# The SiLU after the convolutions: one ScalarE operation in place of tanh and a product

## The chip, the cores and the metric

One NeuronCore of a Trainium2 chip runs the whole program: TensorE (PE: matmuls), VectorE (DVE), ScalarE (ACT: functions through tables), GpSimd (POOL), and SyncE (SP), which issues the DMAs. The metric is the device time of one execution, in microseconds.

## The reference

Two layers on 1024 tokens of width 512: gated linear attention, a router that mixes expert biases, a state-space mixer with a depthwise convolution, and low-rank adapters. The change is in the mixer's convolution:

```python
hBC = proj[..., INTER:INTER + CONV_DIM]          # INTER 8192, CONV_DIM 8192 + 2048
xc = conv_general_dilated(transpose(hBC), conv_w, ..., feature_group_count=CONV_DIM)   # 4 taps, causal
xc = xc + conv_b[None, :, None]
hBC = jax.nn.silu(transpose(xc))                  # silu(x) = x * sigmoid(x)
hs = hBC[..., :INTER]                             # 128 heads of 64: the x channels
Bm, Cm = ...                                      # 8 groups of 128 each: the B and C channels
Y = scores(Cm, Bm) * decay @ (hs * dt) + ...      # in chunks of 128 tokens
out = grouped_rms(Y * silu(gate)) @ out_proj_w
```

## The kernel before

Every matrix product in fp32 is three passes over a high and a low part: ScalarE copies a weight chunk to `slab_hi` (`split_hi`, L190), VectorE subtracts to get `slab_lo` (`split_lo`, L199 or L201), and TensorE runs 12 matmuls of 128x512 per unit (`unit`, L216 to L218). Each engine executes its own list in order. Semaphores tie the lists together: `wait_ge` on one side, `then_inc` on the other.

A convolution of a unit (128 channels, 512 tokens) is `conv_start` on ScalarE (L1182: the fourth tap and the bias, from PSUM to an `acc` buffer) and then three operations of VectorE (`conv_taps`, L1192), each of which adds a tap. The weights and bias are halved on their way in, so that `acc` holds x/2. SiLU(x) is then acc * (1 + tanh(acc)): a tanh on ScalarE into a second buffer, and a product either on VectorE (one operation, L1268, L1625) or on GpSimd (two operations, L1279 and L1282, L1671 and L1674).

`bc_phase` (B and C channels) has 32 units: a loop of two turns, in each two slabs of eight units. The products of even units are on GpSimd, those of odd ones on VectorE. Its results go to DRAM (`bc_scratch`), and the mixer starts after the last of these stores.

`mixer_phase` runs over 8 groups (a loop of 7 turns, and the last written out), each in two halves s = 0 and s = 1, each half in 24 slots. Slots 0 to 7 project and convolve the x units (x0 to x7); slots 8 to 23 project gates and outputs. In slots 4 to 11, TensorE transposes the eight convolved units (L1433) and ScalarE copies each from PSUM to `mx_HS` (L1525); the transposes of slot n + 1 wait for the copy of slot n. From slot 8 on, ScalarE also computes the decays: for two banks a Relu (L1534) and an Exp (L1536), which VectorE multiplies (L1615). It also computes the gate's tanh (L1551) and, for the norm, a Square (L1519). In slots 1 to 8, ScalarE's list has the tanh of the previous slot's unit at the slot's end (L1563). Six of the products in a half are on GpSimd, the last two on VectorE.

Of the kernel before, what the change touches and what calls it, by code (L numbers as in the profile page):

```python
# [59 lines left out]
def alone(eng):  # L60


    eng.nop(nofuse=True)
# [26 lines left out]
def build(nc, d, out):  # L90
# [76 lines left out]
    + ["bc_ld", "bc_a", "bc_tap", "bc_th", "bc_p", "bc_cm", "bc_st0", "bc_st1", "bc_st2", "bc_st3"]  # L167
    + ["mx_ld", "mx_zero", "mx_set", "mx_bc", "mx_row0", "mx_row1", "mx_a", "mx_tap", "mx_th", "mx_cm", "mx_hsT", "mx_pt", "mx_hs",
# [1027 lines left out]
def bc_phase(nc, K, d, scratch):  # L1196
# [6 lines left out]
    th = [mem.enter_context(nc.sbuf_tensor(f"bc_th{i}", [P, HALF], F32)) for i in range(2)]  # L1203
# [30 lines left out]
    def _(act):  # L1234
        with act.Fori(0, 2) as i:
            for j in range(2):
                for u in range(9):
# [9 lines left out]
                    if u > 0:  # L1247
                        act.wait_ge(S["bc_tap"], HEAD + 3 * n)
                        act.wait_ge(S["bc_cm"], HEAD + n - 2)
                        nc.scalar.activation(th[(u - 1) % 2][:, :], acc[(u - 1) % 4][:, :], ACT.Tanh).then_inc(S["bc_th"], 1)  # L1250

    @block.vector
    def _(dve):
        with dve.Fori(0, 2) as i:
            for j in range(2):
                for u in range(9):
# [7 lines left out]
                    if u > 0 and u % 2 == 0:  # L1264
                        dve.wait_ge(S["bc_th"], HEAD + n)
                        dve.wait_ge(S["bc_cm"], HEAD + n - 1)
                        a = acc[(u - 1) % 4][:, :]
                        nc.vector.scalar_tensor_tensor(a, th[(u - 1) % 2][:, :], 1.0, a, ALU.add, ALU.mult).then_inc(S["bc_cm"], 1)  # L1268

    @block.gpsimd  # L1270
    def _(pool):
        with pool.Fori(0, 2) as i:
            for u in range(0, 16, 2):
                n = 16 * i + u
                pool.wait_ge(S["bc_th"], HEAD + n + 1)
                pool.wait_ge(S["bc_cm"], HEAD + n)
                alone(pool)
                a, w = acc[u % 4][:, :], th[u % 2][:, :]
                nc.gpsimd.tensor_tensor(w, w, a, ALU.mult).then_inc(S["bc_p"], 1)  # L1279
                pool.wait_ge(S["bc_p"], HEAD + 8 * i + u // 2 + 1)  # L1280
                alone(pool)
                nc.gpsimd.tensor_tensor(a, w, a, ALU.add).then_inc(S["bc_cm"], 1)  # L1282
# [4 lines left out]
def mixer_phase(nc, K, d, rows, scratch, dtk, from_start, to_end, out):  # L1287
# [17 lines left out]
    POOL_SILU = 6  # L1305
# [6 lines left out]
    with ExitStack() as mem:  # L1312
# [13 lines left out]
        th = sb("th", [P, HALF])  # L1326
# [6 lines left out]
        TH = [th, TO]    # L1333
# [165 lines left out]
        def _(act):  # L1499
            act.wait_ge(S["mx_set"], HEAD + 1)  # L1500

            def half(g, s, last):
                q = 2 * g + s
                n, u0, m = N + 3 * q, U + SLOTS * q, T + NT * q
                for sl, (kind, i) in enumerate(units):
# [50 lines left out]
                    if 1 <= sl < 9:  # L1556
                        act.wait_ge(S["mx_tap"], HEAD + 3 * (NT * q + sl))
                        act.wait_ge(S["mx_cm"], HEAD + NT * q + sl - 2)
                        if sl == 1:
                            act.wait_ge(S["mx_q"], HEAD + NT * q)  # L1560
# [347 lines left out]
```

## Time and profile before

| | us |
|---|---|
| median of 3 runs | 2725.96 (2719.48 to 2730.78) |
| the profiled execution | 2725.1 |
| its span | 2723.4 |
| TensorE busy | 2566.6 |
| VectorE busy | 1877.7 |
| GpSimd busy | 1460.6 |
| ScalarE busy | 1349.5 |
| B/C stage, about | 995 to 1100 |
| mixer, about | 1100 to 2610 |

The profile is that of one execution. TensorE is the busiest engine, and each other engine is busy for half to two thirds of the span. The B/C stage is where TensorE has its longest run of waits for VectorE. A half of the mixer takes about 94 us. Numbers behind a row in brackets are idle time of the engine just before, and who ended it.

### The profile page before, as it was taken

The page shows a single profiled execution, that of the slowest core. Times are in us where ns is not written, and L with a number is a line of the kernel's source. Part 1 is how long each engine was busy: PE and PEld are TensorE (multiplying, and loading weights), DVE is VectorE, ACT ScalarE, POOL GpSimd, SP SyncE. Part 2 cuts the span into 40 slices and gives each one's busy share as a digit, 9 for nine tenths or more (in the row PEclk, how much of TensorE's full clock was granted, in tenths as well). Part 3 has the DMA queues.
Part 4 walks back from the last instruction along what each step waited for, and adds up shares of the span by engine and source line. Part 5 has one row for each costly group of instructions (what it writes and reads, how often), then busy time and mean ns, then how long its engine had stood idle before and what let it go on. Part 6 is the DMA issues. An engine that isn't in the chain of part 4 may idle for free.

```text
span 2723.4 us, 59094 instructions
## 1 busy us (share of the span) xinstructions
PE 2566.6 (94%) x19678; PEld 2041.8 (75%) x19678; DVE 1877.7 (69%) x2744; ACT 1349.5 (50%) x2481; POOL 1460.6 (54%) x1428
## 2 busy tenths in 40 slices
PE   4999999999999679799999999999999999999989
PEld 3778787787787456677777777777777777777777
DVE  5675666766757679757667777587576677775874
ACT  3434434434334255456564664665565646656621
POOL 1654655556546113457556656576575566575720
PEclk8999999999999879899999999999999999999999
DMA  2010010110110023211111111101111111111011
GB/s 89 24 50 29 32 46 24 40 40 23 47 36 12 15 93 112 72 45 38 50 33 58 34 42 50 36 31 50 45 37 51 33 54 34 45 49 38 18 47 47
DMA packets 72663, 119.04 MB, mean 44 GB/s; under 512 B 10310, under 2 KB 22214, under 8 KB 72373
## 3 DMA queue, kind: packets, MB, share of 16 engines
q1 hardware_dynamic: 72388, 115.61, 12.9%
q8 instruction: 144, 2.36, 0.4%
q14 instruction: 131, 1.07, 0.1%
HBM read 102.92 MB, written 12.65 MB: 42 GB/s over the span
## 4 chain that ended last, share of the span: by engine, by line
PE 47%; DVE 4%; issue 4%; POOL 2%; ACT 2%; DVEq 0%; ACTq 0%; POOLq 0%; DMA 0%; SPq 0%
PE proj L216 10%; PE proj L218 10%; PE proj L217 10%; PE core_y L1406 5%; PE core_o L1412 2%; PE turned L250 2%; DVE mx_acc L1192 2%; PE turned L1433 2%; PE decay L1465 1%; PE mx_decay L1465 1%; POOL mx_acc L1674 1%; PE mx_decay L216 1%; PE mx_decay L217 1%; PE mx_decay L218 1%; POOL mx_th L1671 1%
## 5 line engine op out<-in xcount | busy, mean ns | idle before, releaser
L216 PE MATMUL proj<-slab_hi,XTL 128*128 128x512 f32 x816 | 354.6, 435 | 0.0
L199 DVE TENSOR_TENSOR slab_lo<-slab_raw,slab_hi 128x512 fp32r<-128x512 f32 (+2 forms) x272 | 256.8, 956 | 133.5 <-ACT slab_hi L190 108.1
L216 PE MATMUL proj<-XTH,slab_lo 128*128 128x512 f32 x736 | 299.6, 407 | 44.8 <-PEq L81 18.5
L218 PE MATMUL proj<-slab_hi,XTH 128*128 128x512 f32 x816 | 320.2, 392 | 0.0
L217 PE MATMUL proj<-slab_lo,XTH 128*128 128x512 f32 x816 | 318.4, 390 | 0.0
L218 PE MATMUL proj<-XTH,slab_hi 128*128 128x512 f32 x736 | 291.9, 397 | 0.0
L217 PE MATMUL proj<-XTL,slab_hi 128*128 128x512 f32 x736 | 291.4, 396 | 0.0
L1688 POOL TENSOR_TENSOR mx_gate<-mx_gate,mx_hd 128x512 f32<-128x512 f32 x128 | 171.2, 1337 | 156.0 <-DVE mx_hd L1602 145.0
L216 PE MATMUL proj<-slab_hi,mx_otl 128*128 128x512 f32 x576 | 242.0, 420 | 0.0
L218 PE MATMUL proj<-slab_hi,mx_oth 128*128 128x512 f32 x576 | 227.7, 395 | 0.0
L217 PE MATMUL proj<-slab_lo,mx_oth 128*128 128x512 f32 x576 | 227.2, 394 | 0.0
L951 POOL TENSOR_TENSOR at_ropeA<-at_ropeA,at_ropeB 128x512 f32<-128x512 f32 x80 | 110.6, 1383 | 206.6 <-DVE at_ropeB L896 206.6
L190 ACT ACTIVATE slab_hi<-slab_raw 128x512 fp32r<-128x512 f32 (+2 forms) x272 | 151.5, 576 | 111.8 <-PE proj L218 72.0
L216 PEld LDWEIGHTS proj<-XTH,slab_lo 128*128 128x128 f32 x736 | 141.3, 192 | 82.6 <-issue 31.0
L1671 POOL TENSOR_TENSOR mx_th<-mx_th,mx_acc 128x512 f32<-128x512 f32 x48 | 62.1, 1293 | 238.2 <-ACT mx_th L1563 238.1
L216 PEld LDWEIGHTS proj<-slab_hi,XTL 128*128 128x128 f32 x816 | 154.2, 189 | 40.4 <-issue 1.7
L218 PEld LDWEIGHTS proj<-slab_hi,XTH 128*128 128x128 f32 x816 | 153.1, 188 | 34.9
L258 ACT ACTIVATE mx_oth<-turned 128x512 fp32r<-128x512 f32 x144 | 85.8, 596 | 185.7 <-PE turned L250 185.7
L217 PEld LDWEIGHTS proj<-slab_lo,XTH 128*128 128x128 f32 x816 | 153.7, 188 | 30.7
L1192 DVE SCALAR_TENSOR_TENSOR mx_acc<-proj,conv_w,mx_acc 128x510 f32<-128x510 f32 (+2 forms) x192 | 142.9, 744 | 38.5 <-ACT mx_acc L1182 27.7
L218 PEld LDWEIGHTS proj<-XTH,slab_hi 128*128 128x128 f32 x736 | 140.8, 191 | 31.3
L217 PEld LDWEIGHTS proj<-XTL,slab_hi 128*128 128x128 f32 x736 | 141.4, 192 | 27.6
(353 smaller groups left out, 6750.3 us busy)
## 6 DMA issues: line engine op xcount, KB each, us to landing
slab_raw<-in_w_gate SPq DMA_DIRECT2D x64, 256.0 KB, 3.0
slab_raw<-in_w_out SPq DMA_DIRECT2D x64, 256.0 KB, 3.0
slab_raw<-in_w_x SPq DMA_DIRECT2D x60, 256.0 KB, 3.6
slab_raw<-in_w_q SPq DMA_DIRECT2D x32, 256.0 KB, 3.0
slab_raw<-in_w_g SPq DMA_DIRECT2D x32, 256.0 KB, 3.0
slab_raw<-in_w_o SPq DMA_DIRECT2D x32, 256.0 KB, 2.9
bc_scratch<-bc_acc SPq DMA_DIRECT2D x32, 256.0 KB, 2.0
slab_raw<-in_w_bc SPq DMA_DIRECT2D x20, 256.0 KB, 4.3
```

The source lines that it names most:

```text
L190: nc.scalar.activation(K.SH[par][:, c, 0:width], K.RAW[c][:, 0:width], ACT.Copy, scale=scale).then_inc(K.hi_done, 1)
L199: op = nc.vector.tensor_tensor(K.SL[par][:, c, 0:width], K.RAW[c][:, 0:width], hi, ALU.subtract)
L216: nc.tensor.matmul(to[:, 0:bh.shape[-1]], al, bh, start=(c == 0), stop=False)
L217: nc.tensor.matmul(to[:, 0:bh.shape[-1]], ah, bl, start=False, stop=False)
L218: mm = nc.tensor.matmul(to[:, 0:bh.shape[-1]], ah, bh, start=False, stop=(c == KC - 1))
L250: tr = nc.tensor.transpose(K.PT[:, r * P:(r + 1) * P], src[:, r * P:(r + 1) * P], K.ident[:, :])
L258: nc.scalar.activation(K.OTH[t % 2][:, :, :].rearrange("p r n -> p (r n)"), K.PT[:, :], ACT.Copy).then_inc(K.ot_hi, 1)
L951: nc.gpsimd.tensor_tensor(ropeA[q % 3][:, :], ropeA[q % 3][:, :], ropeB[q % 2][:, :], ALU.add).then_inc(S["at_sum"], 1)
L1192: nc.vector.scalar_tensor_tensor(a[:, :, k:], x[:, :, 0:SEQ - k], taps[3 - k], a[:, :, k:], ALU.mult, ALU.add).then_inc(tap, 1)
L1406: mm = nc.tensor.matmul(K.PY[part, h * P1:(h + 1) * P1], M[(2 * t + h // 4) % 4][:, h % 4, part], XCH[t % 2][:, h, :], start=True, stop=True)
L1671: nc.gpsimd.tensor_tensor(w, w, a, ALU.mult).then_inc(S["mx_pt"], 1)
L1688: nc.gpsimd.tensor_tensor(GT[t % GRING][:, :], GT[t % GRING][:, :], HD[t % 2][:, :], ALU.mult).then_inc(K.y_ready, 1)
```

## The change

SiLU becomes one operation of ScalarE in place, `Silu` with scale 2 (the scale undoes the halving), behind the taps. The second buffers, their semaphores and the products of VectorE and GpSimd go; the Square of the gate writes to a scratch of its own. In the mixer the eighth Silu of a half, whose tanh was at the end of slot 8, stands in slot 8 ahead of the decays.

```diff
--- before.py
+++ after.py
@@ -1200,7 +1200,6 @@
     N, U = K.slab, K.unit
     mem = K.mem
     acc = [mem.enter_context(nc.sbuf_tensor(f"bc_acc{i}", [P, HALF], F32)) for i in range(4)]
-    th = [mem.enter_context(nc.sbuf_tensor(f"bc_th{i}", [P, HALF], F32)) for i in range(2)]
     block = K.block
     first_block = 2 * INTER // 2 // P
     banks = [K.PJ[0], K.PJ[1], K.PY, K.PO]
@@ -1246,8 +1245,7 @@
                         conv_start(nc, act, acc[u % 4], banks[u % 4], K.CW[:, ds(blk + u % 4, 1), 3], K.CB[:, ds(blk + u % 4, 1)], S["bc_a"])
                     if u > 0:
                         act.wait_ge(S["bc_tap"], HEAD + 3 * n)
-                        act.wait_ge(S["bc_cm"], HEAD + n - 2)
-                        nc.scalar.activation(th[(u - 1) % 2][:, :], acc[(u - 1) % 4][:, :], ACT.Tanh).then_inc(S["bc_th"], 1)
+                        nc.scalar.activation(acc[(u - 1) % 4][:, :], acc[(u - 1) % 4][:, :], ACT.Silu, scale=2.0).then_inc(S["bc_cm"], 1)
 
     @block.vector
     def _(dve):
@@ -1261,25 +1259,6 @@
                     if u < 8:
                         dve.wait_ge(S["bc_a"], HEAD + n + 1)
                         conv_taps(nc, dve, acc[u % 4], banks[u % 4], [K.CW[:, ds(blk + u % 4, 1), k] for k in range(3)], S["bc_tap"], 3 * n)
-                    if u > 0 and u % 2 == 0:
-                        dve.wait_ge(S["bc_th"], HEAD + n)
-                        dve.wait_ge(S["bc_cm"], HEAD + n - 1)
-                        a = acc[(u - 1) % 4][:, :]
-                        nc.vector.scalar_tensor_tensor(a, th[(u - 1) % 2][:, :], 1.0, a, ALU.add, ALU.mult).then_inc(S["bc_cm"], 1)
-
-    @block.gpsimd
-    def _(pool):
-        with pool.Fori(0, 2) as i:
-            for u in range(0, 16, 2):
-                n = 16 * i + u
-                pool.wait_ge(S["bc_th"], HEAD + n + 1)
-                pool.wait_ge(S["bc_cm"], HEAD + n)
-                alone(pool)
-                a, w = acc[u % 4][:, :], th[u % 2][:, :]
-                nc.gpsimd.tensor_tensor(w, w, a, ALU.mult).then_inc(S["bc_p"], 1)
-                pool.wait_ge(S["bc_p"], HEAD + 8 * i + u // 2 + 1)
-                alone(pool)
-                nc.gpsimd.tensor_tensor(a, w, a, ALU.add).then_inc(S["bc_cm"], 1)
     K.slab += 4
     K.unit += 32
 
@@ -1302,7 +1281,6 @@
     slab_of = {"x": 0, "g": 1, "o": 2}
     out_slot = {t: OFF + GATE_OUT.index(("o", t)) for t in range(NT)}
     HW = HH1 * P1
-    POOL_SILU = 6
     COLS = 4
     gain = 1.0 / (INTER // G1)
     XT_PREV = [0, 0, 0, 1, 2, 3, 4, 5]
@@ -1323,14 +1301,13 @@
         CBM = sb("CBM", [P, NT, P])
         CBO = sb("CBO", [P, NB, P])
         acc = [sb(f"acc{i}", [P, HALF]) for i in range(3)]
-        th = sb("th", [P, HALF])
+        SQ = sb("sq", [P, HALF])
         M = [sb(f"m{i}", [P, 4, P]) for i in range(4)]
         XCH = [sb(f"xch{i}", [P, HH1, P1]) for i in range(2)]
         XD = [sb(f"xd{i}", [P, HH1, P1]) for i in range(2)]
         TO = sb("to", [P, HW])
         HD = [sb(f"hd{i}", [P, HW]) for i in range(2)]
         acc.append(HD[1])
-        TH = [th, TO]  
         GT = [sb(f"gate{i}", [P, SLAB]) for i in range(GRING)]
         K.OTH = [sb(f"oth{i}", [P, KC, P], F32R) for i in range(2)]
         K.OTL = [sb(f"otl{i}", [P, KC, P], F32R) for i in range(2)]
@@ -1499,6 +1476,10 @@
         def _(act):
             act.wait_ge(S["mx_set"], HEAD + 1)
 
+            def silu(q, i):
+                act.wait_ge(S["mx_tap"], HEAD + 3 * (NT * q + i + 1))
+                nc.scalar.activation(acc[i % 4][:, :], acc[i % 4][:, :], ACT.Silu, scale=2.0).then_inc(S["mx_cm"], 1)
+
             def half(g, s, last):
                 q = 2 * g + s
                 n, u0, m = N + 3 * q, U + SLOTS * q, T + NT * q
@@ -1515,8 +1496,7 @@
                         if s == 0 and t == 0:
                             act.wait_ge(S["mx_rs"], HEAD + 3 * NT * g)
                         act.wait_ge(S["mx_q"], HEAD + NT * q + t)
-                        act.wait_ge(S["mx_cm"], HEAD + NT * (q + 1))
-                        nc.scalar.activation(TH[0][:, :], GT[t % GRING][:, :], ACT.Square,
+                        nc.scalar.activation(SQ[:, :], GT[t % GRING][:, :], ACT.Square,
                                              accum_out=SSQ[:, s, t:t + 1]).then_inc(S["mx_q"], 1)
                     if 4 <= sl < 12:
                         u = sl - 4
@@ -1527,6 +1507,8 @@
                     if s == 0 and sl == 8:
                         act.wait_ge(S["mx_a"], HEAD + 3 * g + 3)
                         nc.scalar.activation(CBO[:, :, :].rearrange("p b n -> p (b n)"), K.PO[:, :], ACT.Copy).then_inc(S["mx_bt"], 1)
+                    if sl == 8:
+                        silu(q, 7)
                     if r in SCORE1:
                         t = SCORE1.index(r)
                         for k in range(2):
@@ -1553,14 +1535,8 @@
                         act.wait_ge(K.unit_done, HEAD + u0 + sl + 1)
                         act.wait_ge(S["mx_x"], HEAD + NT * g)
                         nc.scalar.activation(ACC[:, i, :], K.PJ[sl % 2][:, :], ACT.Copy).then_inc(S["mx_acc0"], 1)
-                    if 1 <= sl < 9:
-                        act.wait_ge(S["mx_tap"], HEAD + 3 * (NT * q + sl))
-                        act.wait_ge(S["mx_cm"], HEAD + NT * q + sl - 2)
-                        if sl == 1:
-                            act.wait_ge(S["mx_q"], HEAD + NT * q)
-                        if sl == 2:
-                            act.wait_ge(S["mx_sum"], HEAD + NB * q)
-                        nc.scalar.activation(TH[(sl - 1) % 2][:, :], acc[(sl - 1) % 4][:, :], ACT.Tanh).then_inc(S["mx_th"], 1)
+                    if 1 <= sl < 8:
+                        silu(q, sl - 1)
             with act.Fori(0, G1 - 1) as g:
                 for s in range(2):
                     half(g, s, False)
@@ -1603,8 +1579,6 @@
                         if t % 2:
                             dve.wait_ge(S["mx_pof"], HEAD + NB * q + b + 1)
                             dve.wait_ge(K.y_ready, HEAD + m + t - 2 + 1)
-                            if t == 1:
-                                dve.wait_ge(S["mx_cm"], HEAD + NT * (q + 1))
                             nc.vector.tensor_tensor(TO[:, :].rearrange("p (h n) -> p h n", h=HH1), K.PO[:, :].rearrange("p (h n) -> p h n", h=HH1),
                                                     bc(from_start[:, b, ds(HH1 * q, HH1)], [P, HH1, P1]), ALU.mult).then_inc(S["mx_to"], 1)
                     if r in SCORE1:
@@ -1618,11 +1592,6 @@
                         dve.wait_ge(S["mx_p"], HEAD + NT * q + i + 1)
                         blk = 4 * q + i % 4
                         conv_taps(nc, dve, acc[sl % 4], XB[i], [K.CW[:, ds(blk, 1), k] for k in range(3)], S["mx_tap"], 3 * (NT * q + i))
-                    if 1 + POOL_SILU <= sl < 9:
-                        dve.wait_ge(S["mx_th"], HEAD + NT * q + sl)
-                        dve.wait_ge(S["mx_cm"], HEAD + NT * q + sl - 1)
-                        a = acc[(sl - 1) % 4][:, :]
-                        nc.vector.scalar_tensor_tensor(a, TH[(sl - 1) % 2][:, :], 1.0, a, ALU.add, ALU.mult).then_inc(S["mx_cm"], 1)
                     if last and s == 1:
                         for t in XT_AT.get(sl, ()):
                             tile_xt_lo(nc, K, dve, "d", t, XTB[t])
@@ -1663,15 +1632,6 @@
                 heads = ds(HH1 * q, HH1)
                 for sl in range(SLOTS):
                     r = sl - OFF
-                    if 1 <= sl < 1 + POOL_SILU:
-                        pool.wait_ge(S["mx_th"], HEAD + NT * q + sl)
-                        alone(pool)
-                        a = acc[(sl - 1) % 4][:, :]
-                        w = TH[(sl - 1) % 2][:, :]
-                        nc.gpsimd.tensor_tensor(w, w, a, ALU.mult).then_inc(S["mx_pt"], 1)
-                        pool.wait_ge(S["mx_pt"], HEAD + POOL_SILU * q + sl)
-                        alone(pool)
-                        nc.gpsimd.tensor_tensor(a, w, a, ALU.add).then_inc(S["mx_cm"], 1)
                     if last and s == 1 and sl == OFF + 12:
                         tiles_rstd(nc, K, pool, "d", 0, ve)
                     if r in YSLOT:
```

The list of semaphore names shrinks too (not shown). ScalarE evaluates functions from a table set; an ACT_TABLE_LOAD in its list changes the set.

ScalarE at the head of the mixer's loop, from the first `slab_hi` copy to the SiLU of the first unit (`mx_acc0`) before and after it. Before:

```order
L190 ACTIVATE slab_hi0<-slab_raw0 128x512 [waits unit_done]
L1541 REGISTER_ALU
L1542 ISA [waits unit_done]
L1182 ISA [waits mx_hsT]
L1182 ACTIVATE mx_acc0<-proj0,conv_b,conv_w 128x512
L1541 REGISTER_ALU
L1182 ISA [waits unit_done,mx_hsT]
L1182 ACTIVATE mx_acc1<-mx_decay1,conv_b,conv_w 128x512
L1557 ISA
L1558 REGISTER_ALU [waits mx_tap]
L1563 ACTIVATE mx_th<-mx_acc0 128x512 [waits mx_q,mx_cm]
```

With the change:

```order
L190 ACT_TABLE_LOAD
L190 ACTIVATE slab_hi0<-slab_raw0 128x512 [waits unit_done]
L1523 REGISTER_ALU
L1524 ISA [waits unit_done]
L1182 ISA [waits mx_hsT]
L1182 ACTIVATE mx_acc0<-proj0,conv_b,conv_w 128x512
L1523 REGISTER_ALU
L1182 ISA [waits unit_done,mx_hsT]
L1182 ACTIVATE mx_acc1<-mx_decay1,conv_b,conv_w 128x512
L1480 ISA
L1481 ACT_TABLE_LOAD
L1481 ACTIVATE mx_acc0<-mx_acc0 128x512 [waits mx_tap]
```

Two table loads have come in. The one for Silu stands behind `conv_start` of the second unit and ahead of the operation that holds the wait for the taps.

ScalarE in slot 8, from the first decay to the end of the slot (before), and from the eighth Silu to the gate's tanh (after). `mx_hd1` is the buffer of the eighth unit, `decay` and `mx_decay1` the two banks. Before:

```order
L1533 ISA
L1534 ACTIVATE decay<-decay 128x512 [waits mx_d]
L1536 ACTIVATE decay<-decay 128x512 [waits mx_rl]
L1533 REGISTER_ALU
L1534 ACTIVATE mx_decay1<-mx_decay1 128x512 [waits mx_d]
L1536 ACTIVATE mx_decay1<-mx_decay1 128x512 [waits mx_rl]
L1549 REGISTER_ALU
L1550 REGISTER_ALU [waits unit_done]
L1551 ACTIVATE mx_gate0<-proj0 128x512 [waits turned]
L1557 ISA
L1558 REGISTER_ALU [waits mx_tap]
L1563 ACTIVATE mx_to<-mx_hd1 128x512 [waits mx_cm]
```

With the change:

```order
L1480 ISA
L1481 ACTIVATE mx_hd1<-mx_hd1 128x512 [waits mx_tap]
L1515 ISA
L1516 ACTIVATE decay<-decay 128x512 [waits mx_d]
L1518 ACT_TABLE_LOAD
L1518 ACTIVATE decay<-decay 128x512 [waits mx_rl]
L1515 REGISTER_ALU
L1516 ACTIVATE mx_decay1<-mx_decay1 128x512 [waits mx_d]
L1518 ACTIVATE mx_decay1<-mx_decay1 128x512 [waits mx_rl]
L1531 REGISTER_ALU
L1532 REGISTER_ALU [waits unit_done]
L1533 ACTIVATE mx_gate0<-proj0 128x512 [waits turned]
```

The work on `mx_hd1` has moved from behind the gate's tanh to the front, and a load stands between the first Relu and its Exp.

VectorE in the B/C stage, from the third tap of the third unit (`bc_acc2`) to the first tap of the fourth. Before:

```order
L1191 REGISTER_ALU
L1192 ISA [waits bc_tap]
L1192 SCALAR_TENSOR_TENSOR bc_acc2<-core_y,conv_w,bc_acc2 128x2x253
L1268 SCALAR_TENSOR_TENSOR bc_acc1<-bc_th1,bc_acc1 128x512 [waits bc_cm,bc_th]
L196 REGISTER_ALU
L199 TENSOR_TENSOR slab_lo0<-slab_raw3,slab_hi0 128x512 [waits hi_done]
```

With the change:

```order
L1191 REGISTER_ALU
L1192 ISA [waits bc_tap]
L1192 SCALAR_TENSOR_TENSOR bc_acc2<-core_y,conv_w,bc_acc2 128x2x253
L196 REGISTER_ALU
L199 TENSOR_TENSOR slab_lo0<-slab_raw3,slab_hi0 128x512 [waits hi_done]
```

The product is gone, and nothing has moved past it.

## Rows read from the trace of the kernel before

**Rows 1.** the page's span and busy times, one row for the whole program

```profile
span 2723.4 us, 59094 instructions
...
PE 2566.6 (94%) x19678; PEld 2041.8 (75%) x19678; DVE 1877.7 (69%) x2744; ACT 1349.5 (50%) x2481; POOL 1460.6 (54%) x1428
```

**Rows 2.** waits of TensorE, 1109 to 2610 us: who waited for whom, total, times, longest

```profile
PE turned L1433 <- POOL mx_acc L1674: 9.9, 7, 4.3
...
PE turned L1433 <- ACT mx_HS L1525: 8.4, 16, 1.0
```

**Rows 3.** timeline: start us, us, engine, line, operation [idle before <-releaser]

```profile
33.00 0.42 ACT L534 ACTIVATE dte<-dtd 128x256 f32<-128x256 f32 x1 [0.49 <-DVE dtd L579]
33.43 1.28 ACT L536 ACT_TABLE_LOAD   x1
34.73 0.42 ACT L536 ACTIVATE dtd<-dtw 128x256 f32<-128x256 f32 x1
```

**Rows 4.** timeline of VectorE in the B/C stage, 990 to 1040 us

```profile
1010.34 2.30 DVE L1192 SCALAR_TENSOR_TENSOR bc_acc<-proj,conv_w,bc_acc 128x510 f32<-128x510 f32 x3
...
1018.19 2.31 DVE L1192 SCALAR_TENSOR_TENSOR bc_acc<-core_o,conv_w,bc_acc 128x510 f32<-128x510 f32 x3
...
1021.48 0.69 DVE L1268 SCALAR_TENSOR_TENSOR bc_acc<-bc_th,bc_acc 128x512 f32<-128x512 f32 x1 [0.98 <-POOL bc_acc L1282]
1022.09 0.69 DVE L199 TENSOR_TENSOR slab_lo<-slab_raw,slab_hi 128x512 fp32r<-128x512 f32 x1
...
1028.16 1.29 DVE L199 TENSOR_TENSOR slab_lo<-slab_raw,slab_hi 128x512 fp32r<-128x512 f32 x1
...
1035.44 2.30 DVE L1192 SCALAR_TENSOR_TENSOR bc_acc<-proj,conv_w,bc_acc 128x510 f32<-128x510 f32 x3
```

**Rows 5.** timeline of ScalarE, same stretch, the slab's end

```profile
1021.14 0.62 ACT L190 ACTIVATE slab_hi<-slab_raw 128x512 fp32r<-128x512 f32 x1
```

**Rows 6.** timeline of TensorE, last matmuls of the first two units

```profile
995.47 0.40 PE L218 MATMUL proj<-XTH,slab_hi 128*128 128x512 f32 x1
...
998.21 0.39 PE L218 MATMUL proj<-XTH,slab_hi 128*128 128x512 f32 x1
```

**Rows 7.** timeline, s = 0, the first turned unit, 1865 to 1872 us

```profile
1867.15 0.63 ACT L1563 ACTIVATE mx_th<-mx_acc 128x512 f32<-128x512 f32 x1 [0.95 <-DVE mx_acc L1192]
...
1869.37 1.77 POOL L1674 TENSOR_TENSOR mx_acc<-mx_th,mx_acc 128x512 f32<-128x512 f32 x1
...
1871.27 0.65 PE L1433 MATMUL turned<-ident,mx_acc 128*128 128x128 f32 x4 [0.68 <-POOL mx_acc L1674]
```

**Rows 8.** timeline, s = 1, the second turned unit, 1962 to 1969 us

```profile
1962.28 1.61 DVE L199 TENSOR_TENSOR slab_lo<-slab_raw,slab_hi 128x512 fp32r<-128x512 f32 x1
...
1966.44 0.63 ACT L1563 ACTIVATE mx_th<-mx_acc 128x512 f32<-128x512 f32 x1 [1.28 <-DVE mx_acc L1192]
...
1968.21 0.63 PE L1433 MATMUL turned<-ident,mx_acc 128*128 128x128 f32 x4 [0.93 <-ACT mx_HS L1525]
```

**Rows 9.** timeline, s = 0, from unit x7 to slot 10

```profile
1886.25 0.78 ACT L1182 ACTIVATE mx_hd<-core_y,conv_b,conv_w 128x512 f32<-128x512 f32 x1 [1.43 <-PE core_y L218]
...
1887.06 2.31 DVE L1192 SCALAR_TENSOR_TENSOR mx_hd<-core_y,conv_w,mx_hd 128x510 f32<-128x510 f32 x3 [0.59 <-ACT mx_hd L1182]
...
1889.02 0.60 ACT L1534 ACTIVATE decay<-decay 128x512 f32<-128x512 f32 x1
1889.65 0.58 ACT L1536 ACTIVATE decay<-decay 128x512 f32<-128x512 f32 x1
...
1892.86 0.60 ACT L1525 ACTIVATE mx_HS<-turned 128x512 f32<-128x512 f32 x1
...
1893.65 0.60 PE L1433 MATMUL turned<-ident,mx_acc 128*128 128x128 f32 x4
```

**Rows 10.** timeline, s = 1, the same places

```profile
1978.15 0.78 ACT L1182 ACTIVATE mx_hd<-core_y,conv_b,conv_w 128x512 f32<-128x512 f32 x1 [1.41 <-PE core_y L218]
...
1985.02 0.63 PE L1433 MATMUL turned<-ident,mx_acc 128*128 128x128 f32 x4 [0.20 <-ACT mx_HS L1525]
```

More of the change, by code:

```diff
@@ L166 @@
        "at_mask", "at_y", "at_th", "at_gate", "at_yg", "at_sq", "at_ss", "at_p", "at_x", "at_rl"]
-    + ["bc_ld", "bc_a", "bc_tap", "bc_th", "bc_p", "bc_cm", "bc_st0", "bc_st1", "bc_st2", "bc_st3"]
-    + ["mx_ld", "mx_zero", "mx_set", "mx_bc", "mx_row0", "mx_row1", "mx_a", "mx_tap", "mx_th", "mx_cm", "mx_hsT", "mx_pt", "mx_hs",
+    + ["bc_ld", "bc_a", "bc_tap", "bc_cm", "bc_st0", "bc_st1", "bc_st2", "bc_st3"]
+    + ["mx_ld", "mx_zero", "mx_set", "mx_bc", "mx_row0", "mx_row1", "mx_a", "mx_tap", "mx_cm", "mx_hsT", "mx_hs",
        "mx_pof", "mx_cb", "mx_bt", "mx_d", "mx_e", "mx_m", "mx_xc", "mx_hd", "mx_xd", "mx_y", "mx_yb",
```

## The prediction

> **What bounds the kernel now.** I read the page's busy times first: TensorE is busy 2566.6 of 2723.4 us, ScalarE half the time [rows 1]. Then the waits of TensorE in the mixer (1109 to 2610 us). They are few: 9.9 us for GpSimd's SiLU of a first unit, and 8.4 us for ScalarE's copy `mx_HS` (16 times, in eight pairs of about 0.93 and 0.20) [rows 2]. So in the mixer a step off TensorE counts only where TensorE stands within a microsecond of waiting for it. The B/C convolutions before it are different: there VectorE runs without a gap and TensorE waits for `bc_tap`. The reader should see the same sixteen halves of the mixer as two kinds, s = 0 and s = 1; I read one of each (1861 to 1894 and 1955 to 1985).
>
> The profiled execution took 2725.1 us, 1.7 more than its span; the median shown is 2725.96. The sum is made against 2725.1.
>
> **What the change adds that the diff does not show.** In the order of ScalarE's instructions the new kernel has an ACT_TABLE_LOAD wherever Silu follows tanh or exp, or the reverse: before the first Silu and before the first Exp of each half (32), one more at the head of each of the 7 turns of the mixer's loop, and two in each of the 2 turns of the B/C loop: 43 more than now. The trace prices one: the operation before starts at 33.00 and ends at 33.42, the load begins at 33.43, lasts 1.28, and the next operation starts at 34.73 [rows 3]. I take 1.30 us from the end of one operation to the start of the next.
>
> The Trainium skill (ScalarE: Activation LUTs, What ACT_TABLE_LOAD costs) gives 1.28 us for the load and 1.38 more for a drain, 2.66 together; the trace agrees on the first and shows no gap for the second. With its 2.66, counted in full, the sum below would come out about 22 us higher. That is rival 2, whose own price I make from rows.
>
> **Part 1, the B/C convolutions (one ScalarE operation for two, no VectorE or GpSimd product).** VectorE is the bound: eight units repeat after 1035.44 - 1010.34 = 25.1 us [rows 4], while TensorE can turn out a unit every 998.21 - 995.47 = 2.74 us, or 21.9 for eight [rows 6]. Per eight units go:
> - three of the four products, 0.61 us from start to start (1021.48 to 1022.09): 1.8;
> - at the slab's end, the last tap ends at 1018.19 + 2.31 = 1020.50 and the next slab_lo starts at 1022.09, after 0.98 of waiting for GpSimd and the fourth product: 1.59. Now ScalarE does Silu where tanh was, its slab_hi still starts at 1021.14 and ends at 1021.76 [rows 5], so slab_lo starts at about 1021.8: 1.3. That saves 0.3. The dependence on ScalarE replaces the one on GpSimd;
> - a slab_lo that overlaps a GpSimd product takes 1.29 instead of 0.69: 0.6 to 0.9.
>
> That is about 2.8 per eight units; 25.1 - 2.8 = 22.3 stays above TensorE's 21.9, so all of it counts. Four times 2.8 is 11.2, plus 0.6 since the last store waits for one Silu, not for a tanh, a wait and a product. Against it stand the loads: one at the loop's head before the first slab_hi, partly covered by TensorE's first units (about half of it counts: 0.5), and one at the second turn, exposed (1.3). The loads before the first Silu carry no wait of their own and run while VectorE does the taps. Part 1: -10.0.
>
> **Part 2, the first turned units of a half.** In s = 0, TensorE waits 0.7 for GpSimd's second product, which ends at 1869.37 + 1.77 = 1871.14 [rows 7]. ScalarE stands idle for 0.95 before that tanh at 1867.15; there the load runs now, ahead of the wait for the taps, from 1866.2 to 1867.5. Silu ends at 1868.1, TensorE is ready at 1871.27 - 0.68 = 1870.6, and the wait goes. Of the 9.9 us, the one of 4.3 is the mixer's start, where the load at the loop's head stands directly before the first slab_hi and costs 1.3. There 1.30 + 1.77 us and the gaps around them go and 1.3 come: 2.1 saved. The other 5.6 go whole. Sum -7.7.
>
> In s = 1, TensorE waits 0.93 for `mx_HS`, which ScalarE starts only behind a tanh that waited 1.28 for taps, until 1966.44, and a slab_hi copy [rows 8]. Those taps were late because slab_lo took 1.61 beside GpSimd. With GpSimd quiet it takes 0.69 as elsewhere, the taps end about 0.9 sooner, and the wait goes: with eight pairs, about seven of full size, -6.5. Part 2: -14.2.
>
> **Part 3, slot 8: the stretch from unit x7 to the transposes of slot 10.** These need the sixth `mx_HS` copy. Now it ends at 1892.86 + 0.60 = 1893.46, and TensorE starts at 1893.65 without idle time; in s = 1 it waits 0.20 there [rows 9, 10]. The copy is reached by ScalarE's queue alone. In the changed order the eighth Silu stands ahead of the first Relu and must await the taps of x7, and a load stands between Relu and Exp. From conv_start at 1886.25: taps from 1887.06 to 1889.37, Silu at about 1889.55, Relu 0.52 later at 1890.07, which ends 0.60 later, 1890.67; Exp after 1.30 at 1891.98. From the first Exp to the copy there are now 1892.86 - 1889.65 = 3.21, of which the last tanh (0.63, next after 0.53) falls away: 2.68. The copy starts at 1894.67, ends at 1895.27, and TensorE follows 0.14 later, at 1895.40: 1.75 us of waiting. For s = 1 the same chain from 1978.15 gives 1987.30 against 1985.02, 2.28 more. What is hidden behind it is hidden still: the decay products, the gate and slab_lo are needed only after these transposes. Eight of each: 14.0 + 18.2 = +32.2.
>
> **Parts without effect.** Copy, Relu, Identity and Square need no load of their own in the order. The loads at the heads of turns 2 to 7 have ScalarE idle before conv_start. GpSimd loses 224 products of about 1.3 us, for which nobody but the transposes above waited, and no DMA moves except with Part 1. The duration of Silu is not in the trace; ScalarE's forms of this size lie between 0.58 and 0.78 us, and I take the 0.63 of tanh from SBUF. At the ends the sum moves by -0.05 and +0.15 in each of sixteen chains: -1 to +2.4.
>
> **Sum.** 2725.1 - 10.0 - 7.7 - 6.5 + 32.2 = 2733.1 us, 0.3% above the median. A measurement tells 0.5%, or 13.6 us, from no change.
>
> **Rivals.**
> 1. The loads cost nothing on the path, and the change is faster. If ScalarE could take the load while it waits, the chain of part 3 would shrink to 0.45 in s = 0 and 0.98 in s = 1: 11.4 instead of 32.2, and 2712. If the eighth Silu's wait were also covered, 2701. For it: the first load of each half is covered so. Against it: in slot 8 the load stands after a Relu that itself follows the late Silu, with nothing to wait for. Chance 0.12.
> 2. A switch holds ScalarE longer than 1.30 us. The loads in the trace stand between long operations on SBUF; here the one before writes PSUM and the one after reads what it wrote. Doubling the price to 2.6 adds 1.30 to 16 exposed chains, and some 4 us to part 1 and the mixer's start: 2733 + 25 = 2758. It is the skill's 2.66 that makes me give it room. Against it: two loads at 33.43 and its pair cost 1.30 each. It decides from about 1.7 us a switch, where 16 chains reach the 0.5% line. Chance 0.12.
> 3. The 2 us of slot 8 are not made up and make VectorE late once more: its decay products and gates pile up behind Exp, and each half waits another 0.5 to 1 at the second product. 16 x 0.7 = 11: 2744. Against it: by the same arithmetic the gate's product is ready at about 1895.0, and TensorE, which starts its transposes at 1895.4, has them and a product to do before it asks for the gate. Chance 0.14.
> 4. Part 1 does not come: if TensorE's own start or the stores bound the B/C stage, only a few us go, and 2741. Against it: VectorE's only gap in a period is the 0.98 us before the fourth product [rows 4]. Chance 0.05.
>
> The forecast keeps 0.57. Its own range is 2725 to 2740. The range of all cases: from rival 1 I leave out the lower part, from rival 2 all above 2750: 2714 to 2750. Slower by over 0.5% (above 2739.6): rivals 2, 3, 4 mostly, and a little of the forecast: 0.32. Faster (below 2712.3): most of rival 1: 0.09. The rest: 0.59.
>
> **What would show it.** In the profile after: 48 loads of 1.28 us; the second starts of each half with no wait of TensorE on the first unit; a wait of TensorE at the turned units for `mx_HS`, about 2 us each, 16 times, some 32 us in all; VectorE's period in the B/C stage near 22.3; the mixer's start about 10 us sooner and its length about 18 longer. I am wrong if slot 8's wait is below 1 us or above 3, or if the B/C stage shortens by less than 6.

## The result and the profile after

The changed kernel takes 2742.56 us (median of 6 runs, 2739.32 to 2747.65), the kernel before 2723.65 on the same chip (6 runs). The ratio is 1.007, with a 95% interval from 1.0058 to 1.0081: slower by 18.9 us. The forecast was 8 us slower, so the direction of its likeliest case held, and 11 us are missing (9.5 if the time is set against the forecast's own 2733.1).

The page of the changed kernel, its span and busy times (before: [rows 1]):

```profile
span 2740.6 us, 58214 instructions
...
PE 2575.3 (94%) x19678; PEld 2049.3 (75%) x19678; DVE 1806.3 (66%) x2696; ACT 1402.6 (51%) x2524; POOL 1149.1 (42%) x1204
```

VectorE lost 71 us of work and GpSimd 311, and the time rose by 17 in span. TensorE's work is the same 19678 matmuls, yet it is busy for 8.7 us more. That is the first sign that something other than a wait has grown.

The table loads, from the groups of instructions by line (times, total, mean ns):

```profile
L1481 ACT ACT_TABLE_LOAD x16 | 20.5, 1283 | 0.3
L1518 ACT ACT_TABLE_LOAD x16 | 20.5, 1283 | 0.3
L190 ACT ACT_TABLE_LOAD x10 | 12.8, 1283 | 32.9 <-DVE mx_g_rows L1555 13.4 <-issue 10.7 <-PEq L274 6.1
```

With two each of L536, L538 and L1248 these are the 48 that were expected. Now the waits of TensorE from the B/C stage to the end, who waited for whom, total, times, longest (before: [rows 2]):

```profile
PE turned L1410 <- ACT mx_HS L1505: 31.1, 17, 2.4
...
PE turned L250 <- DVE mx_otl L263: 7.8, 8, 1.1
```

The wait for GpSimd's `mx_acc` is gone, and the one for the copy `mx_HS` has grown from 8.4 to 31.1 us. It holds sixteen waits of slot 10, 30.5 us in all: 1.46 us each in the halves of s = 0 (1.44 to 1.48), 2.35 in those of s = 1.

The B/C stage, timeline of VectorE (start, us; in brackets idle time before; before: [rows 4]):

```profile
1009.31 4.52 DVE L1192 SCALAR_TENSOR_TENSOR bc_acc<-proj,conv_w,bc_acc 128x510 f32<-128x510 f32 x6
...
1019.49 0.69 DVE L199 TENSOR_TENSOR slab_lo<-slab_raw,slab_hi 128x512 fp32r<-128x512 f32 x1 [1.22 <-ACT slab_hi L190]
...
1022.74 0.68 DVE L199 TENSOR_TENSOR slab_lo<-slab_raw,slab_hi 128x512 fp32r<-128x512 f32 x1
...
1031.84 4.52 DVE L1192 SCALAR_TENSOR_TENSOR bc_acc<-proj,conv_w,bc_acc 128x510 f32<-128x510 f32 x6
```

Eight units repeat after 1031.84 - 1009.31 = 22.5 us, where they took 25.1, and no slab_lo takes 1.29 us any more. The stage's last SiLU ends at 1087.97; the last product ended at 1097.53 before. From the stage's first `conv_start` to that end it is 91.2 us and was 101.3. Two of the loads in the way are at the second turn of this loop and at the start of the mixer (timeline of ScalarE):

```profile
1041.49 1.28 ACT L190 ACT_TABLE_LOAD   x1
1042.78 0.63 ACT L190 ACTIVATE slab_hi<-slab_raw 128x512 fp32r<-128x512 f32 x1
...
1101.36 1.28 ACT L190 ACT_TABLE_LOAD   x1 [13.39 <-DVE mx_g_rows L1555]
```

Slot 8 to 10 in a half of s = 0, ScalarE from the eighth SiLU to the copy, and TensorE's transposes (before: [rows 9]):

```profile
1892.41 0.63 ACT L1481 ACTIVATE mx_hd<-mx_hd 128x512 f32<-128x512 f32 x1 [0.27 <-DVE mx_hd L1192]
...
1893.54 1.28 ACT L1518 ACT_TABLE_LOAD   x1
1894.84 0.58 ACT L1518 ACTIVATE decay<-decay 128x512 f32<-128x512 f32 x1
...
1897.53 0.60 ACT L1505 ACTIVATE mx_HS<-turned 128x512 f32<-128x512 f32 x1
...
1898.27 0.63 PE L1410 MATMUL turned<-ident,mx_acc 128*128 128x128 f32 x4 [1.46 <-ACT mx_HS L1505]
```

The same in the half of s = 1 that follows (before: [rows 10]):

```profile
1985.09 0.63 ACT L1481 ACTIVATE mx_hd<-mx_hd 128x512 f32<-128x512 f32 x1 [0.76 <-DVE mx_hd L1192]
...
1986.23 1.28 ACT L1518 ACT_TABLE_LOAD   x1
1987.52 0.58 ACT L1518 ACTIVATE decay<-decay 128x512 f32<-128x512 f32 x1
...
1990.21 0.60 ACT L1505 ACTIVATE mx_HS<-turned 128x512 f32<-128x512 f32 x1
...
1990.95 0.77 PE L1410 MATMUL turned<-ident,mx_acc 128*128 128x128 f32 x4 [2.35 <-ACT mx_HS L1505]
1991.65 1.93 PE L1383 MATMUL core_y<-mx_xch,mx_m 128*32 128x64 f32 x64
...
1994.75 0.40 PE L217 MATMUL proj<-slab_lo,XTH 128*128 128x512 f32 x1
```

The chain is the one that the forecast laid out. New is the row behind it: the 64 matmuls of `core_y` take 1.93 us. In the kernel before, the same place reads (timeline of TensorE):

```profile
1985.57 1.10 PE L1406 MATMUL core_y<-mx_xch,mx_m 128*32 128x64 f32 x64
...
1987.28 0.39 PE L217 MATMUL proj<-slab_lo,XTH 128*128 128x512 f32 x1
```

From the transposes to that second slab product it is 1994.75 - 1990.95 = 3.80 us, and was 1987.28 - 1985.02 = 2.26: 1.54 more, with the same instructions and no wait. The windows of that stretch give the reason (stretch, its length, busy times of PE, PEld, DVE, ACT and POOL, then the granted clock as a share of full speed; the last two numbers are the DMA's busy share and GB/s):

```profile
1988.50:1991.00 2.50, 0.15 (x2) 0.08 (x2) 2.18 (x4) 2.47 (x6) 0.00 (x0) 1.00 0.00 0
1991.00:1993.50 2.50, 2.50 (x68) 2.03 (x68) 1.63 (x3) 1.39 (x3) 0.00 (x0) 0.56 0.00 0
1993.50:1996.00 2.50, 2.50 (x13) 1.84 (x10) 1.22 (x2) 1.78 (x4) 1.49 (x2) 0.76 0.02 5
1996.00:1998.50 2.50, 2.50 (x15) 2.01 (x14) 1.26 (x3) 1.49 (x3) 1.29 (x2) 1.00 0.05 12
```

TensorE had stood idle for 2.35 us, and came back at the lower of its two clock levels, 1.2 in place of 2.4 GHz, for nearly all of the next 2.5 us and about half of those that follow. In s = 0, behind 1.46 us, the clock stays at 1.00:

```profile
1898.00:1900.50 2.50, 2.23 (x71) 1.85 (x72) 2.35 (x4) 1.92 (x5) 0.00 (x0) 1.00 0.02 7
1900.50:1903.00 2.50, 2.50 (x12) 2.02 (x11) 1.27 (x3) 2.02 (x4) 2.13 (x2) 1.00 0.04 10
```

A measure for it in all halves is the first product `core_y`, from its first to its last start. In the kernel after it is 0.88 us in the eight halves of s = 0; in those of s = 1 it is 1.62 four times, 1.33, 1.34 and 1.05 once each, and 0.88 in the last. It can catch only a part of the slow stretch: over the 5 us behind each of these waits the mean granted clock is 0.66 in the first seven halves of s = 1, and 1.00 in the last.

### The profile page after: what moved, and what is told of

Its sections match the earlier page's. It is cut to its first block, busy times and chain, and to the rows that moved or that the text cites. A ratio compares the mean times of both kernels' runs of the same rounds, so it can differ in the third digit from the quotient of the medians.

```text
span 2740.6 us, 58214 instructions
## 1 busy us (share of the span) xinstructions
PE 2575.3 (94%) x19678; PEld 2049.3 (75%) x19678; DVE 1806.3 (66%) x2696; ACT 1402.6 (51%) x2524; POOL 1149.1 (42%) x1204
## 4 chain that ended last, share of the span: by engine, by line
PE 52%; DVE 3%; ACT 3%; issue 2%; POOL 0%; ACTq 0%; DMA 0%; DVEq 0%; SPq 0%; POOLq 0%
PE proj L216 11%; PE proj L218 10%; PE proj L217 10%; PE core_y L1383 5%; PE core_o L1389 2%; PE turned L250 2%; PE turned L1410 2%; DVE mx_hd L1192 1%; PE decay L1442 1%; PE core_y L218 1%; PE core_y L216 1%; PE core_y L217 1%; PE mx_decay L216 1%; PE mx_decay L218 1%; PE mx_decay L217 1%
## 5 line engine op out<-in xcount | busy, mean ns | idle before, releaser
L1669 POOL TENSOR_TENSOR mx_xch<-mx_HS,dt 128x512 f32<-128x512 f32 x128 | 141.3, 1104 | 618.2 <-ACT mx_HS L1505 618.2
L216 PE MATMUL proj<-XTH,slab_lo 128*128 128x512 f32 x736 | 299.4, 407 | 40.8 <-PEq L81 16.3
L199 DVE TENSOR_TENSOR slab_lo<-slab_raw,slab_hi 128x512 fp32r<-128x512 f32 (+2 forms) x272 | 219.4, 819 | 141.9 <-ACT slab_hi L190 117.2
```

The lines of the kernel that those rows point to most:

```text
L199: op = nc.vector.tensor_tensor(K.SL[par][:, c, 0:width], K.RAW[c][:, 0:width], hi, ALU.subtract)
L216: nc.tensor.matmul(to[:, 0:bh.shape[-1]], al, bh, start=(c == 0), stop=False)
L1669: nc.gpsimd.tensor_tensor(XCH[t % 2][:, :, :], hs, bc(dtk[:, t, heads], [P, HH1, P1]), ALU.mult).then_inc(S["mx_xc"], 1)
```

## The experiments

The theory behind all of them is the forecast's sum, with one term more: the wait of slot 10 in s = 1 also costs the clock. The kernel before ran beside each: median 2726.83 for the first four, 2723.44 for the others, 15 runs each. An experiment has five runs where no other number is given. The changed kernel's 2742.56 stands beside 2723.65, so for the first four a difference of medians to it comes out 2 to 4 us smaller than one by the ratios. The profiled executions do not have this difficulty: where a sum below needs it, I give the mixer's length in them, from its first unit to the first unit behind it. It is 1512.3 us before and 1538.6 after.

**The B/C stage alone.** In the kernel before, `bc_phase` of the kernel after:

```diff
-                        nc.scalar.activation(th[(u - 1) % 2][:, :], acc[(u - 1) % 4][:, :], ACT.Tanh).then_inc(S["bc_th"], 1)
+                        nc.scalar.activation(acc[(u - 1) % 4][:, :], acc[(u - 1) % 4][:, :], ACT.Silu, scale=2.0).then_inc(S["bc_cm"], 1)
...          (and without the products of VectorE and GpSimd in bc_phase)
```

> Only the B/C stage has the one-operation Silu; the mixer keeps tanh and products. Theory (the B/C stage gains some 9.6 us because VectorE bounded it, the mixer loses some 27 us): the stage ends 9.6 us sooner, one table load of 1.3 us stands at the mixer's start, nothing else moves: 2723.7 - 8.3 = 2715.4 us. Rival (the gain of the B/C stage is given back later, by a colder start of the mixer): 2721 to 2724.

Measured: 2714.53 us, ratio 0.9963 (0.9949 to 0.9976), span 2712.3 against 2723.4. So Part 1 is worth 10 to 12 us, and the whole loss sits in the mixer. The stage itself takes 91.3 us here, 91.2 in the kernel after, and 101.3 before.

**No loads: tanh in SiLU's place.** This kernel computes tanh(x), not SiLU(x), and has the order of the kernel after with no added load:

```diff
-                nc.scalar.activation(acc[i % 4][:, :], acc[i % 4][:, :], ACT.Silu, scale=2.0).then_inc(S["mx_cm"], 1)
+                nc.scalar.activation(acc[i % 4][:, :], acc[i % 4][:, :], ACT.Tanh, scale=2.0).then_inc(S["mx_cm"], 1)
...          (the same in bc_phase)
```

> As the changed kernel, but with tanh in place of Silu in both stages, in place and without the product, so it computes tanh(x) and not x*sigmoid(x): the same operations and waits, and no table load in the two stages. Theory (the load of 1.30 us in slot 8 is the larger part of the new wait, and the wait of 2.35 us lowers TensorE's clock): the waits at the turned unit of slot 10 shrink to 0.3 (s = 0) and 1.05 us (s = 1), no fall of the clock, B/C stage another 1.8 us shorter: 2707 us, 36 below the changed kernel. Rival (the order, the late eighth Silu, is what costs, the loads are hidden): within 8 us of the changed kernel's 2742.6.

Measured: 2709.44 us, ratio 0.9935 (0.9921 to 0.9948). The loads, with all that follows from their waits, are worth 33 us (37 by the ratios; the mixer is 31.4 us shorter than in the kernel after, the B/C stage 1.0). Of TensorE's waits for the copy, the sixteen of slot 10 are left with 0.18 us in s = 0 and 1.07 in s = 1, 10.0 in all, where the kernel before had 1.6. That is what the eighth operation ahead of the decays costs; the rest of this row is other slots, 1.78 of it at the mixer's start:

```profile
PE turned L1410 <- ACT mx_HS L1505: 13.3, 20, 1.8
```

**The copy ahead of the gate.** In the kernel after, slot 9's copy to `mx_HS` moves into slot 8, before the gate's tanh; two operations of ScalarE fewer stand on the chain.

```diff
+            def hs_copy(q, u): ...      (the four lines of the copy)
-                    if 4 <= sl < 12:
+                    if 4 <= sl < 12 and sl != 9:
+                        hs_copy(q, sl - 4)
...
+                    if sl == 8:         (behind the decays)
+                        hs_copy(q, 5)
```

> As the changed kernel, but the mx_HS copy of slot 9 stands in slot 8, ahead of the gate's tanh and of a slab_hi copy (1.09 us earlier in ScalarE's list). Loads and Silu are the same. Theory: the waits in slot 10 shrink from 1.64 to 0.55 and from 2.35 to 1.26 us, 17.4 in all, and with the second one below the size at which the clock fell, 10 more come back: 2715 us, clock of the stretch after the wait 1.00. Rival (the extra 1.5 us of an s = 1 half is not the clock but a product that waits for something else): 2725 us, and the first product in s = 1 still takes 1.6 us.

Measured: 2713.69 us, ratio 0.9956 (0.9943 to 0.997).

```profile
PE turned L1410 <- ACT mx_HS L1482: 14.8, 18, 1.8
```

The waits fell by 31.1 - 14.8 = 16.3 us, but the time by 28.9 (31 by the ratios, 28.6 in the mixer), and the first product is 0.88 us in all sixteen halves. In slot 10 they are now 0.36 us in s = 0 and 1.25 in s = 1. The difference of some 12 fits a clock that no longer falls, though this run changes both at once. The next one does not. (The 1.64 us that the expectations here and of the control name as the wait of s = 0 is how much the slot had lengthened; the wait was 1.46.)

**The wait kept, the clock held up.** In the kernel after, TensorE does eight products of 128x512 into an unused tile of PSUM where it would only wait, in s = 1 ahead of slot 10's transposes. The copy comes no sooner.

```diff
+                    if s == 1 and sl == 10:
+                        for _ in range(8):
+                            nc.tensor.matmul(PX[:, :], K.XTH[:, 0, 0:P], K.XTH[:, 0, 0:SLAB], start=True, stop=True)
```

> As the changed kernel, but in each s = 1 half TensorE does eight more matmuls of 128x512 into a bank that nobody reads (about 1.8 us) while it would wait for the mx_HS copy in slot 10. Theory (the 2.35 us of idle time lower the granted clock, and that costs about 1.4 us in each of 7 halves): the filler fits into the wait, the clock stays at 1.00, the first product takes 0.88 us again: 2742.6 - 10 = 2732.6 us. Rival (not the clock): the time stays at 2742.6 or grows by what the filler adds.

Measured: 2733.16 us (11 runs), ratio 1.0022 (1.0013 to 1.0031), 9.4 below the kernel after. Timeline of TensorE in a half of s = 1, the filler, the transposes and the product:

```profile
1983.51 1.98 PE L1404 MATMUL mx_normed<-XTH 128*128 128x512 f32 x8
1986.02 0.63 PE L1413 MATMUL turned<-ident,mx_acc 128*128 128x128 f32 x4 [0.54 <-ACT mx_HS L1508]
1986.58 1.10 PE L1383 MATMUL core_y<-mx_xch,mx_m 128*32 128x64 f32 x64
```

The filler does nothing for the result and TensorE still ends up waiting for the copy, 0.54 us; but `core_y` is back at 1.10 us. The first product is 0.88 in all halves. From slot 9's transposes to slot 10's it is 5.72 us in both kernels, so the wait is kept. Against the kernel before, slot 10 of s = 1 is longer by 2.15 us in seven halves and 2.18 in one, which is the added wait (2.35 - 0.20) and nothing else, and slot 11 by nothing; in the kernel after these two slots were longer by 3.70 (mean of groups 2 to 7). Here the clock is told apart from the wait: it is worth 9.4 us by the medians, 9.1 in the mixer and 13 by the ratios, which is most or all of the 11 that are missing.

**The control for it.** Six such products, in the halves of s = 0 alone, where the clock had not fallen:

```diff
+                    if s == 0 and sl == 10:
+                        for _ in range(6):
+                            nc.tensor.matmul(PX[:, :], K.XTH[:, 0, 0:P], K.XTH[:, 0, 0:SLAB], start=True, stop=True)
```

> The changed kernel with six products of 128x512 into an unused PSUM tile ahead of slot 10's transposes, in the halves of s=0 alone, where the wait was 1.64 us and the clock had not fallen: a control for the same filler in s=1. Theory (the filler helps only by keeping the clock): no change, 2742.6 within 3. Rival (the filler helps by itself, by place or by its effect on what follows): 8 x 1.2 less, 2733.

Measured: 2742.28 us, ratio 1.0073 (1.0059 to 1.0087): no change. The wait of s = 0 is filled (0.10 us are left of it). In this run the first product was long in six of the eight halves of s = 1, whose waits are again 2.35. The filler by itself gives nothing.

**One load fewer on the path.** In the kernel after, the eighth unit goes by tanh and a product on VectorE at the end of slot 8. The load ahead of slot 8's Exp then moves to where it is covered.

```diff
-                    if sl == 8:
-                        silu(q, 7)
...
+                    if sl == 8:         (at the end of the slot)
+                        act.wait_ge(S["mx_tap"], HEAD + 3 * NT * (q + 1))
+                        act.wait_ge(S["mx_q"], HEAD + NT * q)
+                        nc.scalar.activation(SQ[:, :], acc[3][:, :], ACT.Tanh).then_inc(S["mx_th"], 1)
...          (in VectorE's slot 8, behind its waits; the gate's Square, which shares SQ, waits for this product too)
+                        nc.vector.scalar_tensor_tensor(acc[3][:, :], SQ[:, :], 1.0, acc[3][:, :], ALU.add, ALU.mult).then_inc(S["mx_cm"], 1)
```

> The changed kernel, but unit 7 of each half takes its SiLU by tanh and a VectorE product, so that the load ahead of slot 8's Exp has gone from the path to slot 10; the copy stays behind the gate. Theory (each load on the path is worth its 1.28 us, and a wait of 2.35 us is what the clock fell after): waits of slot 10 near 1.0 to 1.3 in both kinds of half, first product 0.88 in all, 16 x 1.3 less of wait and 10 less for the clock, 5 to 8 back for VectorE's product: 2719 (2713 to 2725). Rival (the clock falls for another reason than the length of the wait): first products of s=1 still 1.3 to 1.6 us, 2728 or more.

Measured: 2723.23 us (11 runs), ratio 0.9997 (0.9988 to 1.0006). The first product is 0.88 in all halves, and slot 10 has lengthened by 1.26 and 1.28 us against the kernel before, in place of 1.64 and 3.11.

```profile
PE turned L1410 <- ACT mx_HS L1506: 22.2, 17, 1.8
```

By sum: 8.9 us of waits and some 10 of clock, 19.3 measured. The wait of slot 10 is 1.07 us in s = 0 and, over what I expected, 1.48 in s = 1; the clock held behind both. So did it at the mixer's start in this run, behind a longer wait of 2.50 us, where in the kernel after it fell behind 2.48 (timelines of TensorE, first this run, then the kernel after):

```profile
1107.29 0.65 PE L1410 MATMUL turned<-ident,mx_acc 128*128 128x128 f32 x4 [2.50 <-ACT mx_acc L1481]
1107.78 1.06 PE L1420 MATMUL core_o<-mx_CT,mx_BT 128*128 128x128 f32 x8
```

```profile
1107.44 1.11 PE L1410 MATMUL turned<-ident,mx_acc 128*128 128x128 f32 x4 [2.48 <-ACT mx_acc L1481]
1108.35 1.91 PE L1420 MATMUL core_o<-mx_CT,mx_BT 128*128 128x128 f32 x8
```

The length of the last wait alone does not decide whether the clock falls.

**Two loads more on the path.** In the kernel after, an Exp and a SiLU of one column each behind the eighth SiLU, on a tile of their own:

```diff
                     if sl == 8:
                         silu(q, 7)
+                        nc.scalar.activation(DY[:, 0:1], K.mhalf[:, 0:1], ACT.Exp)
+                        nc.scalar.activation(DY[:, 1:2], K.mhalf[:, 0:1], ACT.Silu)
```

> The changed kernel with an Exp and a SiLU of one column each behind the eighth unit's SiLU in slot 8, on a small tile of their own: two more function loads in each half on the way to the copy that slot 10 waits for. Theory (a switch costs its 1.28 us and about 0.02): two loads and two one-column operations are 3.0 us, x 16 halves = 48, plus a fallen clock in the halves of s=0 too, 8 x 1.4 = 11: 2800. Rival (a switch costs twice that, 2.66 us): 5.7 x 16 = 91 and 11: 2845. Rival (loads are hidden): 2743.

Measured: 2810.49 us (4 runs), ratio 1.0316 (1.0299 to 1.0332). The waits of TensorE, and the new stretch in ScalarE's timeline:

```profile
PE turned L1411 <- ACT mx_HS L1506: 80.0, 18, 5.4
```

```profile
1926.31 0.63 ACT L1482 ACTIVATE mx_hd<-mx_hd 128x512 f32<-128x512 f32 x1 [0.27 <-DVE mx_hd L1192]
1926.96 1.28 ACT L1513 ACT_TABLE_LOAD   x1
1928.26 0.20 ACT L1513 ACTIVATE mx_dy<-minus_half 128x1 f32<-128x1 f32 x1
1928.46 1.28 ACT L1514 ACT_TABLE_LOAD   x1
1929.76 0.20 ACT L1514 ACTIVATE mx_dy<-minus_half 128x1 f32<-128x1 f32 x1
1929.87 0.58 ACT L1519 ACTIVATE decay<-decay 128x512 f32<-128x512 f32 x1
```

Each load begins 0.02 us behind the end of the operation before it at most, and the next operation starts 1.30 after the load's start. The wait of slot 10 grew from 1.46 to 4.47 us in s = 0 and from 2.35 to 5.36 in s = 1, 3.01 in each: two times 1.30, two operations of 0.20, and no more. The rival with a switch of 2.66 wanted 5.7. The estimate for the time was 10 too low, on the clock's side. Windows behind the same wait (TensorE restarts at 1935.19):

```profile
1935.00:1937.00 2.00, 1.81 (x36) 1.51 (x40) 1.85 (x3) 1.74 (x4) 0.00 (x0) 0.50 0.03 8
1937.00:1939.00 2.00, 2.00 (x49) 1.66 (x42) 0.71 (x2) 0.57 (x1) 0.00 (x0) 0.78 0.00 0
```

The first product is 1.62 us in all sixteen halves. Slots 10 and 11 of s = 0 together took 5.25 us longer than in the kernel after (groups 2 to 7), 3.01 of them wait: the fall cost 2.2 here, where I had put down 1.4.

**Both mends together.** The copy ahead of the gate and the eighth unit by tanh and product, the edits of two experiments above in one kernel.

> The changed kernel with two edits: slot 9's in-place copy by ScalarE moves ahead of the gate (slot 8), and unit 7 of each half takes its SiLU by tanh and a VectorE product, so that no function table is loaded in slots 8 to 10. Theory (Part 3: the wait of slot 10 is made by two loads and what stands ahead of the copy; in the halves of s=1 its 2.35 us also cost the clock): all waits of slot 10 on the copy fall under 0.3 us, the first product of every half lasts 0.88 us; the copy alone measured 2713.7, the halves of s=0 still paid 1.6 us there and the units' later loads are free: 2698 to 2706. Rival (VectorE is the bound of these slots and its added product comes back as a late operand of the second product): 2710 or more.

(With the copy alone the halves of s = 0 paid 0.36 us of wait, not the 1.6 that this expectation gives them.)

Measured: 2704.98 us, ratio 0.9937 (0.9923 to 0.9951), the fastest kernel here: 0.6% below the kernel before, 1.4% below the one after. In slot 10 no wait for the copy is left; what remains elsewhere:

```profile
PE turned L1410 <- ACT mx_HS L1482: 1.1, 3, 0.8
```

VectorE is not the bound of these slots: slot 11 is 0.27 us longer than before, slot 10 no more than 0.06.

## Why the prediction was right in direction and short in size

The time lies outside the forecast's own range (2725 to 2740) and inside the range of all cases (2714 to 2750), whose upper part was there for rivals 2 and 3; neither of them happened. "Slower by over 0.5%", which is what was measured, had a chance of 0.32, and for other reasons. Lengths of slots and halves below are taken from unit start to unit start in the profiled executions; those of a single slot are means over groups 2 to 7.

**The loads.** 48 of 1.28 us at about 1.30 a switch: as said. The Trainium skill's 2.66 us for a switch (ScalarE: Activation LUTs, What ACT_TABLE_LOAD costs) was worth its rival, but its drain of 1.38 shows in no row here, neither in the mixer nor between the operations of one column.

**Part 1** was -10.0. Measured -9.6 by the end of the last SiLU, and -10.1 (101.3 to 91.2) from the stage's own start, which came 0.5 us later in this execution; the period is 22.5 for the 22.3 that I gave. Alone, 10 to 12 us.

**Part 2** was -14.2. The waits for GpSimd's second product are gone whole. Per half, the slot of the first turned unit shortened by 1.15 us in s = 0 and by 0.85 in s = 1, where I had 0.93. At the mixer's start the forecast saved 2.1 of a wait of 4.3; 2.5 of it are left.

**Part 3** held in the waits. In s = 0 slot 10 lengthened by 1.64 us (forecast 1.75), and in s = 1 the wait went from 0.20 to 2.35 (forecast to 2.48): 8 x 1.64 + 8 x 2.15 = 30.3 for the 32.2 of the sum. The step that failed is the last of this part, "For s = 1 the same chain ... 2.28 more": it took the price of the wait for the price of the slot. Slots 10 and 11 of s = 1 lengthened by 3.11 + 0.59 = 3.70 us, of which 2.15 are wait. The other 1.55 are matmuls at half the clock: 1.54 in the rows at 1990. All halves summed, each from the start of its first unit to the start of the next half's:

| | forecast | measured |
|---|---|---|
| halves of s = 0 | +6.3 | +5.0 |
| halves of s = 1 | +11.7 | +21.4 |

The forecast's column is Part 3 less Part 2 by kind of half. In s = 0 the measured +5.0 is +13.1 in slot 10, -8.7 in the slot of the first turned unit and +0.6 elsewhere. The miss of 9.7 in s = 1 is the clock: slots 10 and 11 of its eight halves lengthened by 28.1 us together, 17.2 of them wait and 10.9 slower matmuls. With the filler, which keeps the wait and holds the clock, the halves of s = 1 come out at +12.1, close to the forecast. I had left this term out, though the sum itself had a wait of 2.3 us in it where there was one of 0.2. The Trainium skill warns of it (TensorE: Matmul & The Clock Gate, Part 1: idle time drops the array from 2.4 to 1.2 GHz); the rows agree on the two levels.

**The rivals.** The loads hidden (2712, 2701): no, without them the kernel is 33 us faster. The dearer switch (2758): no, each switch took 1.30 and two more of them 3.0 us. VectorE late at the second product (2744): that the time is near is luck, since the reason is another; slot 11 of s = 0 is unchanged, and where its 0.59 in s = 1 come from is the clock, since with the filler, and with one load fewer, it is -0.01. Part 1 failing (2741): no. What would have shown the forecast wrong, slot 8's wait outside 1 to 3 us or a B/C stage shorter by less than 6, did not happen; the list had no entry for matmuls that take longer.

What stays open: why the clock fell in seven of the eight halves of s = 1 in the one kernel and in six in the control, all with waits of 2.35 us. The first two units that are turned in the mixer show the same over all runs: the granted clock held behind waits of 1.78 us (four runs) and 2.17 (one), was low behind 2.30, 2.32, 2.48 and 2.51, and held behind 2.49, 2.50 and 2.59 (one run each). No run here says what else decides. The kernel before had such a fall too, behind its wait of 4.28 us at the mixer's start, where the clock was 0.50 for the next 4 us.

## What to carry to other kernels

Fusing two functions into one operation can cost more than it saves when the new function lives in another table set: count the loads in the engine's own order, and price only those behind which somebody waits (here the 16 of slot 8, and one or two at the starts of the stages, of 43 added). When a change makes TensorE wait in one piece, price what follows too, since the matmuls behind the wait can run at half the clock; here that was 1.56 us for each of seven waits, and not for the eighth. Before giving up such a change, look for what stands needlessly ahead of the awaited operation: one copy moved past a gate, and one unit of eight left on the old path, turned +0.7% into -0.6%.

## What the runs showed of the hardware

- Where slot 10's waits were 1.48 us or less the granted clock showed no fall; behind 2.35 us it fell in 13 of 16 halves, in the one shown to 0.56 for the next 2.5 us and 0.76 for 2.5 more, worth 1.5 us; behind 4.5 to 5.4 us it fell each time and was worth 2.2 in s = 0.
- Matmuls whose result nobody uses kept the clock at full speed and made the kernel 9.4 us faster; where the clock had not been falling, the same ones changed nothing.
- An ACT_TABLE_LOAD runs ahead of its operation's wait for taps (at 1870.08, while VectorE was on the taps), takes 1.283 us each time, and 0.01 to 0.02 pass before the next operation when that has nothing to wait for.
- VectorE's slab_lo of 128x512 took 0.68 or 0.69 us all sixteen times in the B/C stage of the kernel after, where GpSimd is quiet; beside GpSimd's products it had taken 1.29 there and 1.61 in the mixer [rows 4, 8].
